# A graph-mixing layer on one core: the 128x128 kernel matrices transposed by a DMA from SBUF instead of by TensorE, with the squares moved behind other ScalarE and GpSimd work

## The reference

```python
z_l, z_g, v = h @ W_lang.T, h @ W_grav.T, h @ W_V.T
zn  = z_l / max(norm(z_l), EPS)
A_l = max(zn @ zn.T, 0) * not_eye
d2  = max(sq + sq.T - 2 * z_g @ z_g.T, 0)         # sq: the squared lengths of z_g
A_g = exp(-d2 / (2 * sigma * sigma)) * not_eye
K_l, K_g = (A * adj / max((A * adj).sum(-1), EPS) for A in (A_l, A_g))
K   = w_l * K_l + (1 - w_l) * K_g                 # a 128x128 kernel matrix
out = (K @ v) @ W_O.T
```

## Time and profile before

| | |
|---|---|
| profiled execution, its own time | 1471.27 us |
| span of its instructions | 1469.2 us |
| median of 3 runs | 1471.29 us |
| layer 2 on TensorE | from about 511 to 1092 us |
| busy in the span: PE, DVE, ACT, POOL | 89%, 75%, 56%, 38% |
| granted TensorE clock, mean | 0.951 |

### The profile page before, as it was taken

The page is one execution under the profiler, slowest core; times in us unless marked ns, Lnnn a source line. Parts: engine busy times, 40 slices in busy tenths (PEclk is TensorE's granted clock), DMA queues, the critical chain, the costliest instruction groups (busy, mean ns, idle before and its releaser), DMA issues. The chain is left out here.

```text
span 1469.2 us, 30223 instructions
## 1 busy us (share of the span) xinstructions
PE 1314.1 (89%) x8890; PEld 730.2 (50%) x8920; DVE 1104.4 (75%) x2202; ACT 820.0 (56%) x1364; POOL 562.5 (38%) x864
## 2 busy tenths in 40 slices
PE   6689978999999499999999999999829963999997
PEld 2255554555555255555555555555405642555554
DVE  0498787888888558887888888887759877676665
ACT  4634345777777434555544555555443432677776
POOL 0100126777778401222222222222320010688887
PEclk9899978999999799999999999999959995999999
DMA  9756100000000111111122111111014520122222
GB/s 326 254 173 216 66 8 1 2 0 0 0 0 0 29 29 30 30 30 30 29 39 40 35 29 29 29 29 30 1 49 155 188 69 1 37 85 79 79 81 98
DMA packets 106078, 89.36 MB, mean 61 GB/s; under 512 B 70828, under 2 KB 70956, under 8 KB 106024
## 3 DMA queue, kind: packets, MB, share of 16 engines
q1 hardware_dynamic: 105832, 88.62, 20.2%
q0 software_dynamic: 192, 0.07, 0.0%
HBM read 54.86 MB, written 17.04 MB: 49 GB/s over the span
## 5 line engine op out<-in xcount | busy, mean ns | idle before, releaser
L538 PE MATMUL pair<-unit_lo,unit_hi 128*128 128x512 f16 x512 | 178.0, 385 | 25.5 <-ACT unit_hi L584 22.3
L584 ACT ACTIVATE unit_hi<-kept 128x512 f16<-128x512 f32 x128 | 79.6, 631 | 120.4 <-DVE kept L562 75.8
L1728 POOL TENSOR_TENSOR sq_lo<-sq,sq_hi 128x512 f16<-128x512 f32 x60 | 69.4, 1157 | 191.5 <-ACT sq_hi L1511 191.5
L542 PE MATMUL diag<-unit_hi 128*128 128x128 f16 x512 | 113.2, 221 | 0.0
L540 PE MATMUL pair<-unit_hi 128*128 128x384 f16 (+2 forms) x384 | 106.3, 277 | 0.0
L1260 POOL TENSOR_TENSOR x_all<-x_all,t 128x512 f32 (+1 forms) x64 | 81.2, 1269 | 50.8 <-ACT t L1164 41.2
L562 DVE TENSOR_TENSOR kept<-x_all,sim 128x512 f32<-128x512 f32 x128 | 81.2, 687 | 25.9 <-DMA sim<-rn_rows 25.2
L1292 PE MATMUL po<-an_h,xwh 128*128 128x512 f16 x256 | 98.0, 383 | 0.0
L1293 PE MATMUL po<-an_l,xwh 128*128 128x512 f16 x256 | 98.0, 383 | 0.0
L1294 PE MATMUL po<-an_h,xwl 128*128 128x512 f16 x256 | 97.8, 382 | 0.0
L1087 PE MATMUL po<-an_h,xwh 128*128 128x512 f16 x256 | 97.8, 382 | 0.0
(11 more groups left out here) (374 smaller groups left out, 4102.7 us busy)
## 6 DMA issues: line engine op xcount, KB each, us to landing
sim<-rn_rows SPq DMA_DIRECT2D x128, 256.0 KB, 3.6
x_all<-in_x_dram SPq DMA_DIRECT2D x16, 1024.0 KB, 14.2
out_dram<-x_all SPq DMA_DIRECT2D x64, 256.0 KB, 2.0
weights_a<-in_L_gnn_W_lang_dram SPq DMA_DIRECT2D x1, 1024.0 KB, 11.6
weights_b<-in_L_gnn_W_grav_dram SPq DMA_DIRECT2D x1, 1024.0 KB, 8.1
weights_a<-in_L_gnn_W_O_dram SPq DMA_DIRECT2D x1, 1024.0 KB, 10.3
an_h<-in_L_gnn_W_V_dram SPq DMA_DIRECT2D x1, 512.0 KB, 6.0
an_l<-in_L_gnn_W_V_dram SPq DMA_DIRECT2D x1, 512.0 KB, 7.8
```

Source lines behind the costliest of these rows:

```text
L538: nc.tensor.matmul(pair[i][:], stat, lo[:, r, :], start=first, stop=False, skip_group_check=True)
L542: last = nc.tensor.matmul(diag[:, i * P:(i + 1) * P], stat, stat, start=(first and i == 0), stop=final, skip_group_check=True)
```

## The change

Layer 2 only. K is no longer transposed by TensorE. ACT writes `k_hi` and DVE writes `k_lo`, as halves straight from `gs` in SBUF, into the memory of `dd`; SP issues one DMA transpose per group of both halves (128 x 1024 float16, 256 KB) into a new tile `kT`; K·v reads that tile and waits for the DMA. On ACT the first square goes behind the third `tl_h`, the second behind the fourth, `k_hi` goes between the third and the fourth `tg_h`. On DVE `k_lo` goes between the second and the third `tg_l`. On POOL the masking of `gs` goes ahead of the first square's lo part. The diff, cut to its core:

```diff
             def _(sp):
                 def transposes(s):
+                    if s.live(1):
+                        g = s.at(1)
+                        settle(sp, o_d, g * G, k.idle["sp"])
+                        settle(sp, kt_l, g + 1, k.idle["sp"])
+                        sp.dma_start_transpose(out=kT[:].rearrange("p h j i -> p (h j) i"), in_=kernels).then_inc(kt_in, 16)
+                    if s.live(-1):
...
+                pipeline(sp, NG, 1, 2, transposes, ahead=1)
@@ PE @@
-                        need(pe, kt_l, g)
+                        need(pe, sum_r, g)
...
-                    if s.live(1):
-                        g = s.at(1)
-                        pe.wait_ge(k_r, g + 1)
-                        for j in range(G):
-                            last = nc.tensor.transpose(pkt[:, j * P:(j + 1) * P], gs[:, j * P:(j + 1) * P], k.ident[:])
-                        last.then_inc(kt_d, 1)
...
-                        pe.wait_ge(kt_l, g + 1)
+                        pe.wait_ge(kt_in, 16 * (g + 1))
...
-                            nc.tensor.matmul(work[j][:], kT_hi[:, js], v_hi[:, j, :], start=True, stop=False)
+                            nc.tensor.matmul(work[j][:], kT[:, 0, j, :], v_hi[:, j, :], start=True, stop=False)
...
@@ ACT @@
-                        square(g, 0)
...
-                        for e in range(C):
+                        for e in range(C - 1):
+                            lang_hi(g, e)
+                    if s.live(2):
+                        square(s.at(2), 0)
+                    if s.live(0):
+                        lang_hi(s.at(0), C - 1)
                     if s.live(2):
                         square(s.at(2), 1)
                     if s.live(0):
+                        for e in range(C - 1):
+                            grav_hi(s.at(0), e)
                     if s.live(1):
-                        act.wait_ge(kt_d, g + 1)
-                        nc.scalar.activation(kT_hi[:], pkt[:], ACT.Copy, scale=S_K).then_inc(kt_h, 1)
+                        act.wait_ge(k_r, s.at(1) + 1)
+                        nc.scalar.activation(k_hi, gs[:], ACT.Copy, scale=S_K).then_inc(kt_h, 1)
+                    if s.live(0):
+                        grav_hi(s.at(0), C - 1)
@@ DVE @@
-                        for e in range(C):
+                        for e in range(2):
                             lo(tg_lo[:, e, :], work[e][:], tg_hi[:, e, :], S_EVAC, tg_h, s.at(0) * C + e + 1, tg_l)
                     if s.live(1):
-                        lo(kT_lo[:], pkt[:], kT_hi[:], S_K, kt_h, s.at(1) + 1, kt_l)
+                        lo(k_lo, gs[:], k_hi, S_K, kt_h, s.at(1) + 1, kt_l)
+                    if s.live(0):
+                        for e in range(2, C):
+                            lo(tg_lo[:, e, :], work[e][:], tg_hi[:, e, :], S_EVAC, tg_h, s.at(0) * C + e + 1, tg_l)
@@ POOL @@
-                        square_lo(s, 0)
                     if s.live(1):
                         pool.wait_ge(sum_r, s.at(1) + 1)
                         pool.tensor_tensor(grouped(gs[:], G), grouped(gs[:], G), over(mask[:], G), ALU.mult).then_inc(mask_r, 1)
                     if s.live(2):
+                        square_lo(s, 0)
```

More of the change, by code:

```diff
@@ L1330, in kernel_mix @@
     (xs_hi, xs_lo, xt_in, tl_d, tl_h, tl_l, tg_d, tg_h, tg_l, gl_d, gg_d, tl_c, tg_c, diag_r, dd_r, bc_d, sum_r, mask_r, u_r, e_r,
-     k_r, kt_d, kt_h, kt_l, v_d, v_h, v_l, o_d, o_u, bn_r, mv_r, rs_r, nm_r, ln_r, sq_r, sq_h, sq_l, ns_d, ksm, msk_r, consts,
+     k_r, kt_in, kt_h, kt_l, v_d, v_h, v_l, o_d, o_u, bn_r, mv_r, rs_r, nm_r, ln_r, sq_r, sq_h, sq_l, ns_d, ksm, msk_r, consts,
      diag_pow, unit_ready, cleared) = (
@@ L1335, in kernel_mix @@
             "T_g_done", "T_l_copied", "T_g_shifted", "diag_chain", "diag_ready", "flipped", "G_l_used", "masked_l", "u_ready",
-            "exp_ready", "k_ready", "kT_done", "kT_hi", "kT_lo", "v_done", "v_hi", "v_lo", "out_done",
+            "exp_ready", "k_ready", "kT_in", "k_hi", "k_lo", "v_done", "v_hi", "v_lo", "out_done",
             "out_added", "stats", "moments", "rstd", "shift", "normed", "sq_ready", "sq_hi", "sq_lo", "sums_done", "k_chain",
@@ L1342, in kernel_mix @@
             k.sb(ctx, n, [P, C, N], F16) for n in ("tl_h", "tl_l", "tg_h", "tg_l", "v_h", "v_l"))
-        kT_hi, kT_lo = (k.sb(ctx, n, [P, N], F16) for n in ("kT_h", "kT_l"))
+        kT = k.sb(ctx, "kT", [P, 2, G, P], F16)
         dd, gs, es = (k.sb(ctx, n, [P, N]) for n in ("dd", "gs", "es"))
+        kernels = dd[:].bitcast(F16)
+        k_hi, k_lo = kernels[:, 0:N], kernels[:, N:2 * N]
         xs = (tl_hi, tl_lo)
@@ L1376, in kernel_mix @@
         early = ColumnScales(k, rows_bank, S_SQ, 3, True, [tiles[:, i * N:(i + 1) * N] for i in range(3)])
-        pkt = pbc
         with nc.Block() as block:
@@ L1381, in transposes @@
                 def transposes(s):
[L1382 to L1388, removed]
+                    if s.live(1):
[4 more added lines that the diff above has]
+                    if s.live(-1):
+                        g, slot = s.at(-1), s.slot(-1)
+                        settle(sp, v_d, (g - 1) * G, k.idle["sp"])
+                        for h, ready in enumerate((xs_hi, xs_lo)):
+                            settle(sp, ready, (g + 1) * G, k.idle["sp"])
+                            sp.dma_start_transpose(out=xT[slot][:, h].rearrange("p j d t -> p (j d) t"),
+                                                   in_=xs[h][:].rearrange("p j n -> p (j n)")).then_inc(xt_in, 16)
+                pipeline(sp, NG, 1, 2, transposes, ahead=1)
                 early.store(sp)
@@ L1471, in step @@
                         g = s.at(1)
-                        pe.wait_ge(kt_l, g + 1)
+                        pe.wait_ge(kt_in, 16 * (g + 1))
                         pe.wait_ge(v_l, (g + 1) * G)
                         for j in range(G):
-                            js = slice(j * P, (j + 1) * P)
                             if not isinstance(s.i, int) or s.i < NG:
                                 pe.wait_ge(tg_l, (g + 1) * C + j + 1)
-                            nc.tensor.matmul(work[j][:], kT_hi[:, js], v_hi[:, j, :], start=True, stop=False)
-                            nc.tensor.matmul(work[j][:], kT_hi[:, js], v_lo[:, j, :], start=False, stop=False)
-                            nc.tensor.matmul(work[j][:], kT_lo[:, js], v_hi[:, j, :], start=False,
+                            nc.tensor.matmul(work[j][:], kT[:, 0, j, :], v_hi[:, j, :], start=True, stop=False)
+                            nc.tensor.matmul(work[j][:], kT[:, 0, j, :], v_lo[:, j, :], start=False, stop=False)
+                            nc.tensor.matmul(work[j][:], kT[:, 1, j, :], v_hi[:, j, :], start=False,
                                              stop=True).then_inc(o_d, 1)
@@ L1511, in square, with lang_hi, grav_hi @@
                     nc.scalar.activation(hi, tile, ACT.Copy).then_inc(sq_h, 1)
+                def lang_hi(g, e):
+                    act.wait_ge(tl_d, g * C + e + 1)
+                    nc.scalar.activation(tl_hi[:, e, :], work[e][:], ACT.Copy, scale=S_EVAC).then_inc(tl_h, 1)
+                def grav_hi(g, e):
+                    act.wait_ge(tg_d, g * C + e + 1)
+                    nc.scalar.activation(tg_hi[:, e, :], work[e][:], ACT.Copy, scale=S_EVAC).then_inc(tg_h, 1)
                 def step(s):
@@ L1531, in step @@
                         act.wait_ge(xt_in, 32 * (g + 1))
-                        for e in range(C):
-                            act.wait_ge(tl_d, g * C + e + 1)
-                            nc.scalar.activation(tl_hi[:, e, :], work[e][:], ACT.Copy, scale=S_EVAC).then_inc(tl_h, 1)
+                        for e in range(C - 1):
[4 more added lines that the diff above has]
+                        lang_hi(s.at(0), C - 1)
                     if s.live(2):
@@ L1537, in step @@
                     if s.live(0):
-                        g = s.at(0)
-                        need(act, gg_d, g)
-                        for e in range(C):
-                            act.wait_ge(tg_d, g * C + e + 1)
-                            nc.scalar.activation(tg_hi[:, e, :], work[e][:], ACT.Copy, scale=S_EVAC).then_inc(tg_h, 1)
+                        need(act, gg_d, s.at(0))
+                        for e in range(C - 1):
+                            grav_hi(s.at(0), e)
                     if s.live(1):
-                        g = s.at(1)
-                        act.wait_ge(kt_d, g + 1)
-                        need(act, o_d, g * G)
-                        nc.scalar.activation(kT_hi[:], pkt[:], ACT.Copy, scale=S_K).then_inc(kt_h, 1)
+                        act.wait_ge(k_r, s.at(1) + 1)
+                        nc.scalar.activation(k_hi, gs[:], ACT.Copy, scale=S_K).then_inc(kt_h, 1)
+                    if s.live(0):
+                        grav_hi(s.at(0), C - 1)
                     if s.live(2):
@@ L1551, in step @@
                         g = s.at(0)
+                        need(act, kt_l, g)
```

## The result

The changed kernel takes 1460.69 us (median of 6 runs, 1458.84 to 1464.9) against 1471.34 for the kernel before (6 runs beside it, 1470.66 to 1473.21): a ratio of 0.9928, 95% interval 0.9914 to 0.9943. The forecast was 1461.3. The profiled execution took 1460.59 us, its span is 1458.8 us.

A forecast was written before the change was run, and what follows sets the result against it. TensorE, busy 99% of the time, was taken to set layer 2's pace. The sum was 1471.27 - 11.04 (15 steps) + 1.1 (last group) = 1461.3 us, range 1459.1 to 1469.5.

The forecast's parts named there:

- The steps: Layer 2, steps 1 to 15: nine steps gain 0.94 us each and six 0.43 us each, 11.04 us in all.
- the wait: TensorE's wait for K before its transposes, in nine steps: 1.16 us from projection to `gram_l` there, 0.65 us without it.
- the transposes: Four TensorE transposes of K between projection and `gram_l`: removing them gains 0.43 us in a step without a wait.
- The due times: In step 6, TensorE would need `gram_g`'s input at 729.77 and K·v's at 732.45; K taken 0.95 us earlier.
- The slack of `gram_g`: Last `tg_l` ends at 729.5, about 0.25 us ahead of `gram_g`'s due time of 729.77.
- GpSimd's hold: VectorE instructions with two SBUF tensors stand still while GpSimd works; L1641 would end with the square's remainder at 724.05.
- The transfer: K's 256 KB DMA transpose lands 3.3 us after issue, between 2.25 and 4.9, 0.75 us ahead of K·v's due time.
- The reorder brings nothing: Rival, chance 0.10: GpSimd's remainders hold VectorE, `gram_g` waits 0.7 us in nine steps; 1467.6 us.
- became TensorE's wait: Rival, chance 0.11: DMA lands 4.5 us after issue, K·v waits 0.45 us in each of 15 steps; 1469.3 us.
- The last group: Step 16, whole chain exposed: K 1.5 us earlier, K·v 0.6 us later, with clock +1.1 us, between -1.1 and +3.7.
- The clock's +0.5: Step 16's K·v: without transposes all twelve matmuls might run at the lower clock, 1.0 us; half was taken.
- the forecast's own range: 1459.1 (tail at its best) to 1464.5 us (tail at its worst, or 0.2 us of `gram_g` waiting per step); chance 0.68.

The follow-up runs named there:

- the reorder alone: Squares and mask moved as in the change, K still transposed by TensorE, against the kernel before: 1466.76 us, ratio 0.9971.
- the DMA alone: The changed kernel with the squares and the mask back in their old places: 1468.85 us, ratio 0.9986 against the kernel before.

## Why the prediction was right

- *The steps.* 11.04 us forecast, 11.17 measured, and the split holds: the wait 4.6 us (nine times 0.51 from the earlier trace rows; the reorder alone gave 4.63), the transposes 6.5 (15 times 0.43; 6.54).
- *The due times.* K was to come 0.95 us earlier. Counted from the first addition of the flipped halves, it came 0.84 us earlier: 723.88 less the addition's start at 711.57 is 12.31, against 727.48 - 714.33 = 13.15 before:

```profile
714.33 0.69 DVE L1612 TENSOR_TENSOR gs<-gs,gram_l 128x512 f32<-128x512 f32 x1 [0.33 <-PE gram_g L1444]
```

  The first `tl_l` came 1.21 us earlier by the same count, L1636 (now L1645) took 0.15 us for 0.46, and L1641 gave 0.68 back (next point). The slack of `gram_g` was forecast at 0.25 us: the last `tg_l` ends at 725.60 + 1.28 = 726.88, and `gram_g` began at 724.32 + 2.68 = 727.00, so 0.12. That was nearer to a wait than I would have liked; by these rows a K 0.12 us later would have begun to cost.
- *GpSimd's hold.* L1641 (now L1650) was to end with the square's remainder. It took 0.87 us instead of 0.19 and ended at 721.43, the remainder at 720.26 + 1.15 = 721.41.
- *The transfer.* 3.3 us forecast, 3.0 measured. The Trainium skill's 1309 ns a block ("VectorE: DVE Perf Modes", The three transpose paths) doesn't fit here either: 8 blocks landed in 3.0 us. Its preference for TensorE holds in this kernel for the last group alone, where TensorE is idle and the DMA path made K·v 1.99 us later.
- *The rivals.* "The reorder brings nothing" priced the lost reorder at 0.7 us a step in nine steps; the DMA alone shows 0.78 in nine and 0.2 in a tenth. The transfer never became TensorE's wait before step 16; put 1.2 us later, it did, and a landing of 4.0 us then showed too.
- *The last group* was the mis-sized term: +1.1 forecast, +2.36 measured in the first profile (15.57 + 21.77 - 36.18 = +1.16 in the second; the two differ by the clock of K·v alone). The earlier start of the row sums was right (1.5 us; 1064.95 less the flips' start at 1057.72 is 7.23 us before, now 1052.18 - 1046.48 = 5.70). Unforeseen was that the second square's remainder now falls on the scaling of `gs`: 1.82 us for 0.87. Before the change it ran beside the row sums, which took no longer for it, and was over ahead of the scaling:

```profile
1057.72 0.66 PE L1444 MATMUL gram_l<-ident,gs 128*128 128x128 f32 x4
...
1064.88 1.15 POOL L1728 TENSOR_TENSOR sq_lo<-sq,sq_hi 128x512 f16<-128x512 f32 x1
...
1067.40 0.87 DVE L1646 TENSOR_SCALAR gs<-gs,small 128x128 f32<-128x128 f32 x4
```

  Counted from the flips, the remainder starts 1.16 us later than before (8.32 for 7.16), since the mask now stands ahead of the first remainder, and the scaling is due 1.56 us earlier (8.12 for 9.68), so they meet. I had allowed the hold only for instructions with two tensors in SBUF, and this one reads one. So K came 0.62 us earlier and not 1.5 (ready 10.98 us after the flips, 11.60 before). From K to K·v it took 4.57 us against 2.58, 2.0 more, close to the forecast's 2.1; together +1.37. The clock's +0.5 was half of a guess whose reason was wrong: with the transposes in place K·v was as slow, and 22.99 and 21.77 us for one program show that this 1 us is chance.
- The sum met the total because the last group's missing 1.3 us were balanced by stretches that the change doesn't touch (-1.5 us in layer 3 above all). The exact part of the forecast is the 15 steps; its last microsecond is luck. (The upper end of the forecast's own range, 1464.5, is a little above what its two reasons add up to: 1461.3 + 2.6 = 1463.9 and 1461.3 + 3.0 = 1464.3.)

## What to carry to other kernels

Where one engine is busy without a gap, a transpose taken off it is worth its own time at that engine's pace, but only if the longer path of the replacement ends before the engine's next need: find that due time and the next wait behind it first, since here the same DMA brings 6.5 us in the 15 steps with the reorder and 3.9 without. It loses 2 in the last group either way, so 4.6 and 2.0 are left. The last turn of a pipeline has no cover; what pays inside the loop can cost there, and giving that turn the old path, a busy array and a GpSimd out of the way brought another 5.7 us in the total (1461.36 to 1455.68). When two runs of one program differ as much as the expected effect, compare stretches of the trace instead of totals: the 15 steps repeat to 0.01 us in the six profiles that share them.

## What the runs showed of the hardware

- A DMA transpose of 256 KB within SBUF landed 3.0 us after issue at the median (up to 4.7 among the sixteen of the changed kernel, all but one within 3.6), one of 512 KB 4.5 us. A straight line through the two medians, an estimate from two sizes only, has 1.5 us for each 256 KB and 1.5 us that don't depend on size.
- A VectorE tensor_scalar with one float32 tensor from SBUF to SBUF is held by GpSimd: one of 281 ns took up to 1224 ns beside a 1.15 us GpSimd instruction, and was back to its length when that was moved. Row sums (tensor_reduce) beside such an instruction took their usual 0.68 us. The Trainium skill, "GPSIMD Engine Reference", 1. Specifications, names two cases of contention, two SBUF inputs and a 2-port perf mode; the trace agrees that the first isn't the only one, though it doesn't show the mode.
- After 9 to 14 us in which TensorE was idle, or did no more than four transposes near the end, the twelve matmuls of K·v began at the lower clock (granted 0.50, 0.43 us apart), and the clock rose behind the sixth of them, the seventh, the ninth or not before the last, in two profiles of one program behind the sixth and not before the last. After unread matmuls in the gap (two profiles) they ran 0.22 us apart but for the first, which the one without transposes had 0.27 ahead of the second.
